# Indirect DMAs of the experts' stage without a bounds register; vacant slots scatter to spare rows of their own

## The reference

```
probs = softmax(x @ Wr + br);  gates, ids = top_k(probs, 2)      # 8 experts
cap   = ceil(1.2 * 8192 / 8) = 1229                              # slots of one expert
order = lexsort((-flat_g, flat_ids))                             # per expert, largest gate first
valid = rank < cap                                               # choices past cap are dropped
h     = silu(xg @ W1[e] + b1[e]);  out = h @ W2[e] + b2[e]       # xg: the tokens in the slots
y     = zeros.at[token].add(out * gate)
```

## Time and profile before

| what | us |
|---|---|
| median of 3 runs (872.54 to 875.57) | 875.31 |
| the profiled execution: its time | 874.87 |
| the profiled execution: span of the trace | 873.1 |
| experts' stage, first gather to the first load of the results | 609.60 to 828.54 |

### The profile page before, as it was taken

How to read it: one execution, slowest core, us unless ns; L and a number is a source line. 1 busy time by engine, 2 the same in 40 slices (tenths; PEclk the granted TensorE clock), 3 DMA queues, 4 the chain that set the end, 5 groups by cost and what they waited for, 6 DMA issues and landing times. The chain is left out here.

```text
span 873.1 us, 14642 instructions
## 1 busy us (share of the span) xinstructions
PE 709.1 (81%) x3872; PEld 492.4 (56%) x3872; DVE 608.5 (70%) x2176; ACT 490.8 (56%) x1209; POOL 441.3 (51%) x576
## 2 busy tenths in 40 slices
PE   7657999999999997999999840055698878879994
PEld 3325667777777775698989730023454444444542
DVE  7957999999999993799999888897111211121168
ACT  4864666666667675687877426334243432334257
POOL 7603767667667664233433530000757777777500
PEclk8877999999999998999999955555699998999997
DMA  9930000000000000600000004000322212221197
GB/s 220 382 132 20 1 2 2 2 1 1 2 1 2 2 2 9 186 1 2 2 2 1 2 0 196 0 0 8 94 64 72 75 50 74 75 75 47 40 355 223
DMA packets 50414, 52.92 MB, mean 61 GB/s; under 512 B 7576, under 2 KB 39624, under 8 KB 50080
## 3 DMA queue, kind: packets, MB, share of 16 engines
q1 hardware_dynamic: 44496, 41.62, 14.6%
q0 software_dynamic: 5120, 10.37, 4.2%
q10 hardware_dynamic: 720, 0.05, 0.1%
HBM read 28.04 MB, written 24.18 MB: 60 GB/s over the span
## 5 line engine op out<-in xcount | busy, mean ns | idle before, releaser
L917 DVE SCALAR_TENSOR_TENSOR s_cv<-s_pU,tap_w,s_cv 128x256 f32<-128x256 f32 x372 | 153.4, 477 | 11.1 <-ACT s_cv L848 10.7
L1939 POOL DMA_INDIRECT arena<-token_rows,token_of x80 | 81.1, 1014 | 115.3 <-issue 114.7
L2060 DVE TENSOR_TENSOR arena<-e_pB,e_gate 128x384 f32<-128x384 f32 (+2 forms) x24 | 14.5, 602 | 122.5 <-PE e_pB L1984 122.5
L1947 POOL DMA_INDIRECT choice_rows<-arena,choice_of x80 | 79.6, 995 | 32.9 <-issue 22.6
L2011 ACT ACTIVATE e_h<-e_pH,e_bcols 128x384 f32<-128x384 f32 (+2 forms) x96 | 58.7, 616 | 65.4 <-PE e_pH L1968 63.0
L1968 PE MATMUL e_pH<-e_xgT,e_w 128*128 128x384 f32 (+2 forms) x192 | 82.7, 580 | 0.0
L716 POOL TENSOR_TENSOR s_xa<-s_xt,arena 128x512 f32<-128x512 f32 x32 | 34.4, 1074 | 86.9 <-ACT s_xt L866 86.9
L848 ACT ACTIVATE s_cv<-s_pU,tap_b,tap_w 128x256 f32<-128x256 f32 x124 | 63.5, 560 | 23.3 <-PE s_pU L750 23.0
L750 PE MATMUL s_pU<-arena,w_in 128*128 128x262 f32 x248 | 68.2, 399 | 8.4 <-DVE s_cv L917 3.9
L1976 PE MATMUL e_pO<-e_h,e_w 128*128 128x384 f32 (+2 forms) x192 | 72.7, 522 | 0.4 <-ACT e_oT L2018 0.4
L1492 PE MATMUL m_pM<-w_m,m_h 128*128 128x128 f32 x512 | 62.7, 276 | 0.1
(11 more groups left out here) (308 smaller groups left out, 1874.3 us busy)
## 6 DMA issues: line engine op xcount, KB each, us to landing
choice_rows<-zrow SPq DMA_DIRECT2D x16, 512.0 KB, 8.4
arena<-choice_rows SPq DMA_DIRECT2D x28, 256.0 KB, 5.1
token_rows<-arena SPq DMA_DIRECT2D x8, 520.0 KB, 5.8
n_x<-in_L_attn_x_dram SPq DMA_DIRECT2D x8, 512.0 KB, 7.5
arena<-in_L_attn_x_dram SPq DMA_DIRECT2D x8, 512.0 KB, 4.7
e_w<-in_L_ffn_W_dram SPq DMA_DIRECT2D x16, 256.0 KB, 3.1
out_dram<-arena SPq DMA_DIRECT2D x14, 256.0 KB, 4.2
decay_rows<-arena SPq DMA_DIRECT2D x2, 1024.0 KB, 4.7
```

What stands on the lines that cost most here:

```text
L917: v.scalar_tensor_tensor(out=by_tile(cv[:, p % 2, m, :]), in0=columns(m)[:, :, tap:tap + P], scalar=tap_w[:, m, tap:tap + 1], in1=by_tile( ...
L1939: g.indirect_dma_start(xg[:, n % RING, i, :], None, table, bass.IndirectOffsetOnAxis(ap=token_of[:, c:c + 1], axis=0), bounds_check=TOKENS ...
L1947: g.indirect_dma_start(choice, bass.IndirectOffsetOnAxis(ap=choice_of[:, c:c + 1], axis=0), yo[:, n % RING, i, :], None, bounds_check=2 * ...
```

## The change

The scatter's and the gather's calls lose `bounds_check`. `choice_rows` gets 10240 more rows, one for each slot, and a vacant slot's `choice_of` becomes 16384 + its slot number (a tile `r_beyond`, written by one more iota, supplies it). Nobody reads those rows. In the built program the 160 register moves ahead of the indirect DMAs, and the register operands, are gone.

```
-    choice = nc.dram_tensor("choice_rows", (2 * TOKENS, D), F32, kind="Internal").ap()
+    choice = nc.dram_tensor("choice_rows", (2 * TOKENS + SLOTS, D), F32, kind="Internal").ap()
...
-                zeros = choice.rearrange("(n p r) d -> n p (r d)", p=P, r=8)
+                zeros = choice[0:2 * TOKENS].rearrange("(n p r) d -> n p (r d)", p=P, r=8)
...
+                g.iota(beyond[:, :], [[P, COLS]], base=2 * TOKENS + 1, channel_multiplier=1, allow_small_or_imprecise_dtypes=True)
...
-                link(v.tensor_scalar(vacant[:, :], acc[:, 0, :], 0.0, FAR, ALU.is_equal, ALU.mult))
+                link(v.scalar_tensor_tensor(out=vacant[:, :], in0=acc[:, 0, :], scalar=0.0, in1=beyond[:, :], op0=ALU.is_equal, op1=ALU.mult))
...
                         g.indirect_dma_start(xg[:, n % RING, i, :], None, table,
                                              bass.IndirectOffsetOnAxis(ap=token_of[:, c:c + 1], axis=0),
-                                             bounds_check=TOKENS - 1, oob_is_err=False).then_inc(s_xg[n % RING], 16)
+                                             oob_is_err=False).then_inc(s_xg[n % RING], 16)
...
                         g.indirect_dma_start(choice, bass.IndirectOffsetOnAxis(ap=choice_of[:, c:c + 1], axis=0),
-                                             yo[:, n % RING, i, :], None, bounds_check=2 * TOKENS - 1,
-                                             oob_is_err=False).then_inc(s_scat[n % RING], 16)
+                                             yo[:, n % RING, i, :], None, oob_is_err=False).then_inc(s_scat[n % RING], 16)
```

More of the change, by code:

```diff
@@ L1526, in build @@
             cols, lanes = sbt("r_cols", [P, COLS], BF16), sbt("r_lanes", [P, P], BF16)
-            own = sbt("r_own", [P, 1])
+            own, beyond = sbt("r_own", [P, 1]), sbt("r_beyond", [P, COLS])
             SET = 4
```

## The result

The changed kernel takes 867.97 us (median of 5 runs, 866.28 to 868.25); the kernel before, run beside it, 875.57 (5 runs, 872.54 to 876.55). The ratio is 0.9922 [0.9906, 0.9938], so 6.8 us less [5.4 to 8.2]. That lies inside the predicted range, but it is faster by more than the 0.5% that a measurement can tell: the forecast of no change (873.5) was wrong by 5.5 us, and rival B is the case that came true. The range holds the time only because its lower end was set for B; the likeliest case by itself reached from 870.9 to 879.

The account below looks back on a forecast made before the run. POOL's back-to-back indirect DMAs were taken to bound most of the experts' stage, 135 counting end to end. From 874.87 us, moves -0.09, comparison -1.35 and DVE +0.04 gave -1.40, so 873.5; range 856 to 879.

Parts of the forecast that it names:

- rival B: In every indirect DMA the comparison is dear, 0.029 to 0.14 us each; at 0.10 the time is 861.3; chance 0.43.
- links 1, 3 and 5: Experts' stage: first gathers, 115 DMAs from 640.96, last 10 scatters; POOL sets the pace, 135 DMAs counting.
- 2 and 4: Experts' stage: up to the first result at 640.96, and 798 to 814.7; PE works while POOL waits for results.
- Link 3: Middle of the experts' stage, from the first scatter at 640.96: POOL sets the pace for 115 DMAs, 1.312 us each.
- 20d: Fall of PE's waits in each expert's period: 20 DMAs, each cheaper by d.
- d = 0.01: Saving in us per indirect DMA from dropping the comparison, within 0 to 0.14; over 135 DMAs -1.35 us.
- the threshold of 0.029: Saving in us per indirect DMA above which the time counts as faster, 3.9 us over 135 DMAs.
- the prediction's last sentence: Forecast is wrong if the comparison loops over rows at equal cost for passing and failing rows; equal scatter lengths wouldn't show it.
- the sign given for B: DMA length or the 0.30 us of "issue" gets shorter by the same amount in nearly all 160 DMAs.
- Three moves are 0.09 us: Register moves on the path only where POOL has run dry, before 609.60, 640.96 and 814.72: -0.09 us.
- Rival D: POOL's 0.30 us of "issue" is sequencer work; moves save 0.029 x 135 = 3.9 us, 870.9; inside the forecast's 0.50.
- C: Without a bound each indirect DMA takes a longer way on POOL; at 0.047 us each, 881.2 us; chance 0.07.

Follow-up runs that it names:

- the second timing: The changed kernel timed again beside 11 runs of the kernel before (873.35 us): 867.81 us, ratio 0.9927.
- the greater lag: Changed kernel with scatters issued behind the gathers of the sixth or seventh group after theirs, not the fifth: 862.54 and 861.41 us.
- lag 6: Changed kernel with a group's scatters issued behind the gathers of the sixth group after it, not the fifth: 862.54 us, ratio 0.9865.

## Why the prediction was wrong, by its own steps

**The place was right.** POOL sets the pace in links 1, 3 and 5, PE in 2 and 4. Link 3 follows the DMAs' lengths to within 0.1 us. PE's waits for gathers went from 34.0 us to 31.7, the direction that rival B gave, though less than its 20d in every period.

**The step that failed** is "A comparison that takes no branch is a smaller difference in the work than that. I take d = 0.01, nearer to the 15 ns than to the 140". By the means the bound costs 54 ns in a gather and 16 in a scatter. Over the 68 gathers and 67 scatters of the 135 that is 0.035 us each, 4.7 us, above the threshold of 0.029 at which B begins. The row behind the step was read rightly: a scatter with rows that fail is as long as one without, and the kernel in which none fails shows the same. What doesn't follow is that such a comparison is small. Equal lengths say only that all 128 rows pay alike; the prediction's last sentence named this hole, and the value was still taken from the near side of it. The 15 ns between gathers and scatters were no scale either, since the comparison is part of them: without it the medians are 25 ns apart (944 and 969), with the gather now the shorter. Nor did the sign given for B hold, that all 160 would get shorter by the same amount: the two kinds differ by 38 ns.

**A term that was mis-sized** is "Three moves are 0.09 us". Counting the move's own length misses the DMA's step behind it: the two restarts inside the stage cost 0.5 us each. For the stretch ahead of the first gather no run separates the move from other differences.

**Together**, by measured sizes and with the clock alike: 4.7 + 1.0 - 0.26 = 5.4, against 5.39 in the stage; the timed gains of 6.8 [5.4 to 8.2] and 6.4 us [4.5 to 8.2] hold it at their low end (the medians of the second timing are 5.5 apart). What is above it was not traced further; chance in the clock's rise, 1.8 us when it falls on one side, would be enough for it, but no run shows that it is that.

**Right as they stood:** the moves are hidden wherever POOL has work in its queue (149.78 us in link 3 without them); the vacant rows bring 10.58 MB where 10.57 were forecast, and from the last scatter to the load it is 2.32 us where it was 2.24; DVE's operation became 243 ns; the iota is hidden. The case that the prediction worked out from "DMA: Bandwidth & Descriptors" of the Trainium skill, section "Anatomy of one DMA", that landings set the pace and nothing is gained, is ruled out for this stage by the same runs: what POOL's own work lost came back in the time. Rival D, the moves, gave 870.9, and the kernel with the bounds set once shows nothing of it in link 3. C did not come.

## What to carry to other kernels

Where an engine issues one instruction behind the other with a fixed gap, multiply even a few ns of its instruction by its count before calling an edit free; and where a cost without a row decides at 3% of an instruction, "small" is no number: measure it by itself. Put a wait on the DMA itself and set registers that don't change once, ahead of the loop: an instruction in between costs nothing while the queue is full and 0.5 us at every restart. And after making the bounding engine's work cheaper, look at where it still waits: the greater lag, 5.3 to 6.4 us, gave about as much again as the change.

## What was not expected of the hardware

- The price of a bounds check differs between the two kinds of DMA: 54 ns in a gather of 128 rows, 16 in a scatter, with both bounds gone. In scatters it is the same whether rows pass or fail, in gathers the same for rows of 512 and 520 bytes. The kernels keep the register operand wherever they compare, so the comparison and the reading of its operand aren't told apart, here or above where the text speaks of the comparison's price.
- An indirect DMA behind one of the other kind is longer: first, second and third after the switch, gathers took 1.05, 1.01 and 1.00 us before and 0.99, 0.96 and 0.94 after the change, scatters 1.02, 1.00 and 0.98, then 1.00, 0.98 and 0.97 (means from POOL's timeline, the stage's very first gather left out).
- The time at which PE's granted clock rises at the head of the stage differs between executions of one kernel, 14.4 and 18.6 us behind the first gather, and is worth 1.8 us; over the profiled executions of all runs it lies between 11.8 and 18.7, and it came late in one kernel without any bound too (lag 6, 17.8). Later in the stage the clock dips for a while in every execution, mostly in link 3. In two runs, the one with a step ahead and the one with spare rows checked, the dip fell into link 4 (0.83 from 780 to 790, 0.84 from 790 to 800), where PE sets the pace, and link 4 was 25.75 and 25.56 us there, 1.3 to 1.7 longer than in the kernel before and the changed one, a restart's 0.5 us set aside.
